# A 1 MB load moved ahead of a store on SyncE's queue, in the attention output stage of a transformer layer

## The reference

```python
h = _layernorm(x, axis=-1) * (1 + ca) + sa
x = x + ga * _L0_attn_ref(h, ...)      # linear attention: 16 heads of 32
h = _layernorm(x, axis=-1) * (1 + cb) + sb
x = x + gb * _L0_ffn_ref(h, ...)       # 8 experts, the best 2 for each token

# inside _L0_attn_ref
q, k = relu(q), relu(k)
vk = jnp.einsum('bhen,bhdn->bhed', v_pad, k)      # v_pad has a row of ones
out = jnp.einsum('bhed,bhdn->bhen', vk, q)
out = out[:, :, :-1] / (out[:, :, -1:] + EPS)     # by the denominators
return out @ w_proj.T + b_proj
```

## Time and profile before

| | us |
|---|---|
| median of 3 runs | 2207.81 |
| lowest and highest run | 2203.33, 2214.65 |
| the profiled execution | 2219.13 |
| its span | 2217.2 |

### The profile page before, as it was taken

How to read it: one execution, slowest core, us unless ns; L and a number is a source line. 1 busy time by engine, 2 the same in 40 slices (tenths; PEclk the granted TensorE clock), 3 DMA queues, 4 the chain that set the end, 5 groups by cost and what they waited for, 6 DMA issues and landing times.

```text
span 2217.2 us, 42645 instructions
## 1 busy us (share of the span) xinstructions
PE 2072.3 (93%) x9352; PEld 1636.6 (74%) x9353; DVE 1328.9 (60%) x3194; ACT 830.6 (37%) x1572; POOL 798.3 (36%) x622
## 2 busy tenths in 40 slices
PE   7999999999998888884899999999999999999996
PEld 4888878888765566663688888888878778888885
DVE  7655555565486777764465555655655556556564
ACT  3444444444466666661222222222222222222222
POOL 5676656667325555553111111111111111111111
PEclk9999999999998888886999999999999999999999
DMA  8756555566636666667855558558775875765544
GB/s 271 259 188 204 201 168 172 204 205 197 214 115 220 228 205 208 207 235 252 226 129 126 126 132 238 126 129 236 181 181 129 265 186 128 219 147 131 124 111 81
DMA packets 294089, 404.89 MB, mean 183 GB/s; under 512 B 50904, under 2 KB 189144, under 8 KB 286176
## 3 DMA queue, kind: packets, MB, share of 16 engines
q1 hardware_dynamic: 166272, 258.79, 37.2%
q0 software_dynamic: 30096, 72.12, 15.7%
q10 hardware_dynamic: 97488, 71.77, 10.1%
HBM read 210.57 MB, written 191.98 MB: 182 GB/s over the span
## 4 chain that ended last, share of the span: by engine, by line
PE 47%; DMA 4%; issue 1%; SPq 1%; ACTq 1%; DVE 0%; ACT 0%; POOL 0%; DVEq 0%; POOLq 0%
PE bank L1866 47%; DMA act_rows<-hact 2%; DMA arow<-act_rows 1%; DMA out_rows<-orow,cur_tok 1%; ACTq L1115 0%; DMA wbuf<-expert_split 0%; SPq L582 0%; DMA expert_rows<-rows,dest 0%; ACT x_t_hi L1097 0%; DVE x_t_lo L1712 0%; DVE act_t_lo L1729 0%; DMA meta<-expert_rows 0%; SPq L580 0%; DVE orow L1771 0%; POOL out_rows L810 0%
## 5 line engine op out<-in xcount | busy, mean ns | idle before, releaser
L1866 PE MATMUL bank<-wbuf,x_t_hi 128*128 x2168 | 685.1, 397 | 30.7 <-DVE x_t_lo L1712 27.6
L810 POOL DMA_INDIRECT out_rows<-orow,cur_tok x135 | 209.0, 1548 | 976.1 <-DVE orow L1771 796.0
L1866 PEld LDWEIGHTS bank<-wbuf,x_t_hi 128*128 128x128 f32 x2168 | 411.4, 190 | 128.7 <-issue 32.5
L1866 PE MATMUL bank<-wbuf,x_t_lo 128*128 x1084 | 430.1, 397 | 0.0
L1866 PE MATMUL bank<-wbuf,act_t_hi 128*128 x1072 | 339.8, 398 | 16.5 <-DVE act_t_lo L1729 11.7
L1718 DVE TENSOR_TENSOR hact<-bank,gact 128x512 f32<-128x512 f32 x135 | 93.3, 691 | 381.1 <-PE bank L1866 354.2
L1866 PEld LDWEIGHTS bank<-wbuf,act_t_hi 128*128 128x128 f32 x1072 | 203.2, 190 | 66.7 <-issue 19.6
L1866 PEld LDWEIGHTS bank<-wbuf,x_t_lo 128*128 128x128 f32 x1084 | 205.9, 190 | 48.2
L1866 PE MATMUL bank<-wbuf,act_t_lo 128*128 x536 | 212.9, 397 | 0.0
L1097 ACT ACTIVATE x_t_hi<-bank 128x512 fp32r<-128x512 f32 x135 | 80.9, 599 | 293.2 <-PE bank L1866 278.0
L1121 ACT ACTIVATE act_t_hi<-bank 128x512 fp32r<-128x512 f32 x132 | 79.1, 599 | 288.8 <-DMA arow<-act_rows 233.4
(11 more groups left out here) (231 smaller groups left out, 3887.3 us busy)
## 6 DMA issues: line engine op xcount, KB each, us to landing
wbuf<-expert_split SPq DMA_DIRECT2D x24, 1536.0 KB
act_rows<-hact ACTq DMA_DIRECT2D x135, 256.0 KB
xrow<-expert_rows SPq DMA_DIRECT2D x538, 64.0 KB
arow<-act_rows ACTq DMA_DIRECT2D x536, 64.0 KB
expert_split<-split_hi SPq DMA_DIRECT2D x32, 768.0 KB, 3.4
expert_split<-split_lo SPq DMA_DIRECT2D x32, 768.0 KB, 5.9
q_rows<-qf SPq DMA_DIRECT2D x16, 1024.0 KB, 6.8
qb<-q_rows SPq DMA_DIRECT2D x16, 1024.0 KB, 7.1
```

What stands on the lines that cost most here:

```text
L810: pool.indirect_dma_start(out=out, out_offset=bass.IndirectOffsetOnAxis(cur_tok[at][:, 0:1], 0), in_=orow[at % 2][:, :], in_offset=None, c ...
L1866: last = mm(dst, stationary(a, f), moving(b, f), start=(first and k == 0), stop=(k == parts * n - 1), skip_group_check=not first)
```

## The change

The load of the queries of group g+2 moves from behind the first store of rows to ahead of it, so that it stands right behind the second store of the group before. Everything else stays: the same loads, stores and waits.

```diff
@@ -536,9 +536,9 @@
                 sp.wait_ge(s_x1, TPG * g + (half + 1) * TPG // 2)
                 sp.dma_start(group_rows(out, g)[:, h, :], x1[:, h, :]).then_inc(s_x1st[half], 16)
 
-            store_half(0)
             if has(g, 2):
                 load_q(g + 2, par)
+            store_half(0)
             if g and has(g, 1):
                 sp.wait_ge(s_x1, TPG * g + 3)
                 load_x(g + 1, 1 - par)
```

## The result

| | before | after |
|---|---|---|
| median of the runs made together | 2211.23 us (4 runs, 2203.33 to 2220.43) | 2236.97 us (4 runs, 2230.05 to 2250.62) |
| the profiled execution | 2219.13 us | 2230.29 us |

The ratio is 1.0112, with a 95% interval of [1.0068, 1.0157]: the changed kernel is some 25 us slower, above the 0.5% that a measurement can tell from no change and above the range of the prediction, 2183 to 2230 us. A ratio in this document is worked out from the single runs, less two of the kernel before that ran in a slower state, and need not equal the quotient of the medians exactly. Its span and clock line stand on its page; they answer to the earlier trace rows.

What follows compares the result with a forecast made beforehand. TensorE was taken to bound the second stage, with pauses for lg_t followed by a lower clock. The terms 0 + 0 + 0 - 2.8 us brought the median of 2207.81 us to 2205 us, range 2183 to 2230 us.

Steps and rivals of the forecast that it cites:

- SyncE's own time, 0.: SyncE's queue, second stage: the load's issue fits idle time behind the second store, store_half(0) starts as before; cost 0.
- Who waits for the load, 0.: TensorE's denominators read the load first, late in the group, with no DMA wait; landing 8 us sooner gives 0.
- What it takes from the scatter, -2.8 us.: Load beside GpSimd's scatter of indirect DMAs: moving it ends two late divides, saving 2.8 us.
- two coincidences of a long issue and a divide: Two groups where the load's issue lasted 1.70 and 1.82 us and VectorE's divide began about its end; 2.8 us.
- The rule that I cited: A long load issue on SyncE is a queue waiting, not one holding VectorE; by it 0, not 2.8 us.
- The bounds.: Second-stage groups: at best all like group 14 or 13, 20 or 36 us saved; at worst like group 6, 40 lost.
- rival 2: Disturbance moves to the scatter's start, residual 1 later by 1.3 to 1.5 us in twelve groups: about 2225 us; chance 0.26.
- Rival 1: The load makes the second stage's divides late, so twelve groups lose their delay: 2188 us, at most 2172; chance 0.34.
- The rule of turns.: DMA engines alternate between queues packet by packet, so load and scatter only share them, nobody waits: 2207.8 us.
- The sum: Whole kernel: terms 0 + 0 + 0 - 2.8 us on the median of 2207.81 us, giving 2205 us; chance 0.40.

Runs made afterwards that it cites:

- c1_after: The changed kernel again, unaltered, on an occasion without late hand-overs: 2154.91 us, ratio 1.0001 [0.9974, 1.0028] to the kernel before.
- d1_after: The changed kernel once more, unaltered, on an occasion with late hand-overs: 2236.47 us, ratio 1.0067 [1.0035, 1.01] to the kernel before.
- j1_alone: The kernel before with second-stage query loads cut to 16 KB and each group's first store put off to its end: 2247.02 us, ratio 0.9982.
- the first comparison: The changed kernel against the kernel before, as first measured: 2236.97 us against 2211.23 us, ratio 1.0112.
- the eight sittings: Follow-up sets of runs, each on one chip with the kernel before among them, which took 2155.34 to 2251.24 us.
- d2_early: The kernel before with the query load one group further ahead, behind the load of x, before the second store: 2224.81 us, ratio 1.0023.
- The twice kernel: The changed kernel with a second load of the same 1 MB at the old place; four runs: ratios 0.9993, 0.9986, 0.9994, 1.0001.
- e4_early: Same program as d2_early, query load behind the load of x, one group further ahead than in the kernel before: 2155.32 us, ratio 0.9978.
- the third sitting: Follow-up set with d1_after and d2_early against the kernel before, which took 2224.24 us; it had late hand-overs.

## Why the prediction was wrong

*SyncE's own time, 0.* Right. The load is issued 0.47 us behind the second store, its issue takes 0.34 to 0.42 us, and store_half(0) follows 7.7 us later (743.15).

*Who waits for the load, 0.* Right. The denominators (L1935) of the changed kernel have 7.9 us of "issue" and 0.4 us, once, of the load in their idle time, where they had 7.8 and none. In c1_after, where the trace gives the landing, it is 5.5 to 7.7 us, 6.0 in the median of twelve: about the 5.8 that I took.

*What it takes from the scatter, -2.8 us.* This is the step that failed: it measured +23 us in the pair of traces (12 groups x 1.9 us), and 25 and 15 us by the two ratios (1.0112 and 1.0067). It rested on two coincidences of a long issue and a divide. In the changed kernel no issue of the load is longer than 0.42 us, and the divides are later than before. So the long issue was not what held VectorE. The trace of the kernel before already said so: late first divides stand in six of its groups 3 to 14, and in four of them (3, 8, 10, 11) the issue took 0.44 to 0.46 us. Group 10:

```profile
867.60 0.45 SPq L488 DMA_DIRECT2D qb<-q_rows  x1
...
869.19 0.69 DVE L1355 TENSOR_TENSOR onf<-bank,qb 128x512 f32<-128x512 f32 x1 [1.82 <-PE bank L2012]
```

What the runs show in place of the saving: the divides' releases from TensorE come late in more groups, TensorE pauses more for lg_t and then runs at the lower clock, and the stage gets 21 us longer. Why the load's new place makes more of them late stays open. The rule that I cited from the Trainium skill, "Perfetto Trace Analysis", section on HWDGE DMA instructions, that such a duration contains a wait for the descriptor generator's lock, is not contradicted by these rows: by it this saving was 0, and none came. That the two long issues waited for that lock no run shows.

*The bounds.* I took group 14, "no load beside the scatter", as a sample of a world without the load, and group 6 as the worst. Both were draws. In d1_after group 14, which again has no load, has its first divide at 986.58, after 3.28 us of idle time, and takes 27.8 us; in c1_after every group with a load is on time. One trace held both kinds of group and I read them as best and worst case of the load, when what varies is the hand-over. The result lies between rival 2's 2225 us and its 2248 us (all groups as long as group 6); the range ended at 2230 and left that part out.

*Rival 1, the load at its old place makes the divides late.* Wrong: j1_alone has no large load and the latest divides of all.

*Rival 2, the disturbance moves to the scatter's start.* Nearest, with the right sign and short in size for the first comparison (about 2225 forecast, 2236.97 measured), right in size for the second (15 us). Groups above 26 us were its mark, and came. Its other mark, a "remote" wait at residual 0 or 1, did not, neither in the changed kernel's trace nor in d1_after: the late hand-over is still that of the spread, in the scatter's second half. The mechanism as I put it, that residual 1 comes 1.3 to 1.5 us later in every group, is not what happened; more of the same late divides is. By idle time they cost 12 us more (28 to 40), by length of groups 23: the rest is what a late divide brings behind it, the logits' pause and the lower clock.

*The rule of turns.* In the prediction "DMA: Bandwidth & Descriptors" of the Trainium skill, section on queues, rings and completion order, gave no change. Where hand-overs are on time the runs agree with it (1.0001 [0.9974, 1.0028]); where they are late the time is not what it gave (1.0112 and 1.0067). No run shows whether the turns hold there; in j1_alone the divides are late with no load for the scatter's transfers to share the engines with.

*The frame.* The sum was set against one sitting of the kernel before. Across the first comparison and the eight sittings that kernel took 2155 to 2251 us; three of these nine had late hand-overs. The changed kernel itself was compared in three: slower in the two with late hand-overs, no different in the one without. That the first comparison was one of the former was luck, and the forecast did not reckon with either kind.

What stays open: why some sittings have late hand-overs at all, and by what way a load beside the scatter's start makes more of them. That the changed kernel has more of them is shown by two comparisons, each with one trace, and that d2_early has fewer fits a harm done at the scatter's start; j1_alone, with no large load and all its divides late, shows that such a harm could only be an addition and not the cause. The twice kernel, which would have told whether the second transfer matters, never met a late sitting. None of the versions beats the kernel before: e4_early has 0.9978 [0.9952, 1.0005] in one sitting and 1.0023 [0.9992, 1.0053] in the other.

## What to carry to other kernels

Before pricing a step by "this group has it, that group has not", look whether the difference between the groups is there for the same program in another execution; a repeat of the kernel before on another occasion would have shown 2155 beside 2211 us. A wait marked "remote", behind a matmul that was through microseconds before, is a release that came late, and what moving transfers around it will do can't be forecast until one knows what delays it. Work that stands behind such hand-overs (here the two divides ahead of the logits) may be worth taking out of the stretch in which GpSimd issues indirect DMAs; no run tried that.

## What the runs showed that I had not expected

**A semaphore update of TensorE can come microseconds late beside GpSimd's indirect DMAs, and in steps.** The place of the first divide, measured from the start of the indirect DMA (L789) that was running, falls into few classes. Count of groups 3 to 14, worked out from the timelines:

| first divide begins | before | after | d1_after | d2_early | j1_alone | c1_after |
|---|---|---|---|---|---|---|
| in the 5th indirect DMA or the gap behind it | 6 | 3 | 1 | 4 | 0 | 12 |
| in the 6th, 0.60 to 0.69 us in | 3 | 2 | 2 | 6 | 0 | 0 |
| in the 7th, 0.04 to 0.12 us in | 1 | 2 | 3 | 0 | 0 | 0 |
| in the 7th, 0.74 to 0.94 us in | 2 | 5 | 6 | 2 | 11 | 0 |
| in the 8th | 0 | 0 | 0 | 0 | 1 | 0 |

Two rows of the timeline of d1_after, group 14, where no load stands beside it:

```profile
985.82 0.96 POOL L789 DMA_INDIRECT expert_rows<-rows,dest  x1 [0.30 <-issue]
...
986.58 0.69 DVE L1355 TENSOR_TENSOR onf<-bank,qb 128x512 f32<-128x512 f32 x1 [3.28 <-remote]
```

986.58 is 0.76 us after the start of the 7th indirect DMA; in j1_alone it is 752.54 - 751.70 = 0.84, in the changed kernel's group 5 0.78. The indirect DMAs follow each other every 1.27 us. Measured from the first of them, the divides begin at about 5.8 us when prompt, and when late at about 7.1, 7.8 or 8.5 to 8.7 us. (Two in the first row are late by less, 1.36 us idle in the changed kernel and 0.66 in d2_early, both in group 7.) The wait is not a fixed delay behind the spread: in group 7 of j1_alone the spread ends 0.4 us earlier in the group than elsewhere, and the divide begins at the same place, 8.70 us after the scatter's start, where ten of the others have 8.61 to 8.70. But residual 0 also stands 1.31 us behind the scatter's start in each of these groups, so a fixed place in the scatter is a fixed place in the whole group, and no run shows that it is GpSimd's work that holds the updates.

The divides are not alone. In the kernel before, ScalarE's lg_t and VectorE's residual 2 wait for "remote" too, all in groups whose first divide is prompt (2, 5, 12, 13, 14) or absent (15). The waits of 640 to 1000 us, and the two rows of group 13:

```profile
ACT lg_t L996 <- remote: 8.0, 6, 3.7
...
DVE x L1387 <- remote: 6.7, 6, 2.3
```

```profile
948.83 0.69 DVE L1387 SCALAR_TENSOR_TENSOR x<-bank,xb 128x512 f32<-128x512 f32 x1 [1.02 <-remote]
...
948.92 0.60 ACT L996 ACTIVATE lg_t<-bank 128x512 f32<-128x512 f32 x1 [1.02 <-remote]
```

TensorE's last projection for that residual was through at 946.09 and its logits at 947.07, yet the two engines are released within 0.1 us of each other. So TensorE's updates can come late to both engines, and together. Without group 15, which lies outside this window in the changed kernel, the two sums are 4.4 and 4.3 us before and 2.0 each after: a small part of what the divides idle more, residual 2 and lg_t idle less.

**The same program on the same chip differs by 3 to 4%** between sittings: the kernel before took 2224 us in the third sitting and 2155 in the sixth on one chip, 2160 in the seventh and 2251 in the eighth on another. Within a sitting its median is good to about 0.3%. Only comparisons within one sitting mean anything for this kernel.
